# Experts of a small transformer stack: from every expert on every token to sorted pairs of token and chosen expert

## The reference

```python
comb = jnp.sum(jax.nn.one_hot(top_i, E) * top_w[..., None], axis=2)   # top 2 of E = 8, by a distance to 8 centroids
h = jax.nn.gelu(jnp.einsum('bnd,edf->bnef', x, W1) + b1)              # d = 128, f = 512
y = jnp.einsum('bnef,efd->bned', h, W2) + b2
out = jnp.einsum('bne,bned->bnd', comb, y)
```

## Time and profile before

| | |
|---|---|
| median of three runs | 763.6 us (761.05 to 763.6) |
| profiled execution | span 757.7 us; its own time is not given apart from the three runs |
| PE busy | 660.7 us, 87% of the span |
| DVE, ACT, POOL busy | 514.1, 342.2, 151.8 us |
| attention 0, experts with what is merged into them, attention 1 from its step 1 | 0 to 248.5, 248.5 to 506.7, 506.7 to about 700 us |

### The profile page before, as it was taken

One profiled execution on the slowest core, in us unless ns is written; L12 is line 12 of the kernel. 1 busy time (PEld: TensorE's weight loads), 2 busy tenths in 40 slices (PEclk: granted clock), 3 DMA queues, 4 the chain that ended last, 5 costly groups with the idle time before them and its releaser, 6 DMA issues.

```text
span 757.7 us, 13009 instructions
## 1 busy us (share of the span) xinstructions
PE 660.7 (87%) x5007; PEld 464.5 (61%) x5007; DVE 514.1 (68%) x1313; ACT 342.2 (45%) x472; POOL 151.8 (20%) x145
## 2 busy tenths in 40 slices
PE   1478889999989899999999998999989899998664
PEld 0333556565655699898998785775555655555443
DVE  6578776777743536658537467777786778666993
ACT  1110566656575444433444432335546455674221
POOL 5301010100011010010021301302203010345764
PEclk9995999999999999999999999999999999999985
DMA  5405876454320000000000200211211211000000
GB/s 152 126 22 147 173 218 132 85 141 75 66 55 14 1 1 1 1 1 1 1 1 1 63 1 12 75 23 28 83 42 27 65 45 35 25 12 1 14 15 28
DMA packets 29325, 38.07 MB, mean 50 GB/s; under 512 B 3719, under 2 KB 23185, under 8 KB 29265
## 3 DMA queue, kind: packets, MB, share of 16 engines
q1 hardware_dynamic: 29265, 37.25, 20.3%
HBM read 26.33 MB, written 10.88 MB: 49 GB/s over the span
## 4 chain that ended last, share of the span: by engine, by line
PE 64%; DVE 25%; issue 5%; ACT 3%; POOL 1%; DMA 0%; POOLq 0%; DVEq 0%; ACTq 0%
PE ps L989 14%; PE ps L486 9%; PE ps L444 7%; DVE mx L663 6%; PE ps L465 6%; PE ps L979 4%; PE ps L512 3%; PE ps L981 3%; PE ps L980 3%; DVE xn L926 3%; PE ps L447 2%; ACT pT L557 1%; PE ps L494 1%; PE ps L469 1%; DVE x L1063 1%
## 5 line engine op out<-in xcount | busy, mean ns | idle before, releaser
L663 DVE TENSOR_REDUCE mx<-ps 128x1 f32<-128x384 f32 (+3 forms) x352 | 215.5, 637 | 72.5 <-PE ps L447 70.4
L557 ACT ACTIVATE pT<-ps 128x1024 f32<-128x1024 f32 x160 | 162.1, 1023 | 86.9 <-PE ps L469 71.9
L1024 ACT ACTIVATE pT<-ps,b1c 128x512 f32<-128x512 f32 x128 | 87.8, 687 | 129.6 <-PE ps L981 128.7
L989 PEld LDWEIGHTS ps<-w_sb,pT 128*128 128x128 f32 x1024 | 132.2, 191 | 11.8 <-issue 1.3
L989 PE MATMUL ps<-w_sb,pT 128*128 128x128 f32 x1024 | 135.5, 275 | 0.0
L447 PE MATMUL ps<-mask_qk,identb 128*128 128x128 bf16 (+2 forms) x352 | 90.2, 256 | 0.0
L444 PE MATMUL ps<-stA 96*128 96x128 bf16 (+3 forms) x256 | 69.6, 332 | 19.2 <-DVE mx L663 14.3
L486 PE MATMUL ps<-pT,vA 128*32 128x512 f32 (+3 forms) x1024 | 77.9, 439 | 0.7 <-ACT pT L557 0.7
L1063 DVE SCALAR_TENSOR_TENSOR x<-ps,comb,x 128x128 f32<-128x128 f32 x128 | 36.0, 344 | 58.4 <-PE ps L989 58.3
L444 PE MATMUL ps<-kA,stA 96*128 96x128 bf16 (+3 forms) x256 | 63.7, 304 | 12.8 <-DVE mx L663 11.6
L979 PE MATMUL ps<-x_hi,w_hi 128*128 128x512 f32 x128 | 62.9, 491 | 1.2 <-DVE w_lo L1045 1.0
(11 more groups left out here) (232 smaller groups left out, 964.1 us busy)
## 6 DMA issues: line engine op xcount, KB each, us to landing
stA<-stack_scratch SPq DMA_DIRECT2D x48, 192.0 KB, 3.4
stB<-stack_scratch SPq DMA_DIRECT2D x48, 192.0 KB, 4.5
stack_scratch<-part SPq DMA_DIRECT2D x12, 384.0 KB, 3.2
w_sb<-in_L_ffn_W_dram SPq DMA_DIRECT2D x16, 256.0 KB, 5.6
stack_scratch<-part SPq DMA_DIRECT2D x12, 256.0 KB, 3.1
stack_scratch<-part SPq DMA_DIRECT2D x12, 128.0 KB, 3.1
x<-in_L_attn_z_dram SPq DMA_DIRECT2D x4, 256.0 KB, 4.4
out_dram<-x SPq DMA_DIRECT2D x4, 256.0 KB, 2.3
```

Source lines behind the costliest of these rows:

```text
L557: act.activation(dst_, src, ACT.Exp, scale=SCALE).then_inc(a["ex"], 1)
L663: nc.vector.tensor_reduce(mx[:, g % 2, qb, heads[0]:heads[0] + nh], ps[:, S_BANK[n % 2], 0:nh * w].rearrange("p (h k) -> p h k", h=nh), AX ...
L989: last = pe.matmul(ps[:, ST_BANK[1] + m % 2, f * P:(f + 1) * P], hT[:, (m % 2) * FC + c, f * P:(f + 1) * P], w2_sb[:, e, c, :], start=(c = ...
L1024: act.activation(hT[:, (m % 2) * FC + f, :], ps[:, ST_BANK[0] + n % 2, :], ACT.Gelu, bias=b1c[:, e * FC + f:e * FC + f + 1]).then_inc(M["g ...
```

## The change

The tokens are taken in two halves of 8 tiles (batches 0 and 1, then 2 and 3). Each half has 2,048 pairs of token and chosen expert. They get slots in an order sorted by expert, each expert's slots filled up to a multiple of 128; that is at most 16 + 7 = 23 tiles of 128 slots (`NTL`), and 23 are always run. The place of each pair is computed on DVE and PE ("CNT", "RANK", "POS"), POOL writes the normed tokens to their slots in DRAM by 16 indirect DMAs of 128 rows x 512 B a half ("SCAT"), SP loads the tiles one by one ("XG"), and POOL fetches each token's two results by 16 indirect DMAs a half ("GATH"); "COMB" on DVE adds them to x. A tile is turned ("XTT"), split on DVE, multiplied by W1 of its expert ("H", now with the tokens as the fixed side, and a fourth product for the bias), turned again ("HT") and multiplied by W2 ("Y", with a fifth product for the bias). The expert of a tile is known only on the chip, so PE loads 23 registers a half ("REG") and takes the weights at register addresses. W1 is split once, for all experts, in step 4 of attention 0, which needs W1 through a DRAM copy of 2 MB made at the start; the slots in DRAM are filled once beforehand (1.5 MB). Routing of batch 0 moves into step 3 of attention 0, of batch 1 into step 4, of batches 2 and 3 into the first 12 of the 49 rounds of experts; the weights of the last layer are quantized in rounds 12 to 24. The tail and step 0 of attention 1 stand alone.

```diff
+HALVES = 2
+TH = NT // HALVES
+NTL = 2 * TH + E - 1
+XG, YB = 4, 3
+def routing_order(b):
+    o = [(n, b, 0, 0) for names in ROUTING for n in names]
+    if b % 2:
+        o += [(n, b // 2, 0, 0) for n in ("CNT", "RANK", "POS", "SCAT")]
     return o
+def experts_order():
+    rounds = []
+    last = HALVES * NTL
+    for k in range(-2, last + 1):
+        o = []
+        for hf in range(HALVES):
+            if k + 2 == hf * NTL:
+                o += [("REG", hf, 0, 0)] + [("XG", hf * NTL + n, 0, 0) for n in range(XG)]
+        if k + 2 < last:
+            o.append(("XTT", k + 2, 0, 0))
+        if 0 <= k + 1 < last:
+            o.append(("H", k + 1, 0, 0))
+        if 0 <= k < last:
+            o.append(("HT", k, 0, 0))
+        if k >= 1:
+            o.append(("Y", k - 1, 0, 0))
...
+        for hf in range(HALVES):
+            if k - 1 == (hf + 1) * NTL - 1:
+                o.append(("GATH", hf, 0, 0))
...
+    o += merged(flat(rounds[:12]), of("M", routing_order(2) + routing_order(3)))
...
+    o += merged(flat(rounds[12:NTL + 2]), weights)
+    at = NTL + 2
+    o += flat(rounds[at:at + 4])
+    for t in range(TH):
+        o += rounds[at + 4 + t] + of("M", [("COMB", 0, t, 0)])
...
+    o += merged(flat(rounds[at:]), of("A1", first1[2:]))
+    start = steps1[0].index(("LN", 2, 0, 0))
+    o += of("A1", steps1[0][:start]) + of("M", [("COMB", 1, t, 0) for t in range(NB)]) + of("A1", steps1[0][start:])
...
+            elif name == "REG":
+                pe.wait_ge(M["pos"], b + 1)
+                for k in range(NTL):
+                    tiles[b * NTL + k] = pe.value_load(tid_i[0:1, b, k:k + 1], min_val=0, max_val=(E - 1) * F)
...
+                whi = w_hi[:].rearrange("p e f -> p (e f)")[:, bass.ds(tiles[n], F)]
+                wlo = w_lo[:].rearrange("p e f -> p (e f)")[:, bass.ds(tiles[n], F)]
+                pe.matmul(bank, x_hi[:, n % 2, :], whi, start=True, stop=False)
+                pe.matmul(bank, x_hi[:, n % 2, :], wlo, start=False, stop=False)
+                pe.matmul(bank, x_lo[:, n % 2, :], whi, start=False, stop=False)
+                pe.matmul(bank, hot[:, hf, k:k + 1].broadcast_to([P, P]), b1r[:], start=False, stop=True).then_inc(M["h"], 1)
...
+            elif name == "SCAT":
+                pool.wait_ge(M["pos"], b + 1)
+                pool.wait_ge(ld_fill, 32)
+                if b:
+
+                    pool.wait_ge(M["xtt"], b * NTL)
+                for t in range(TH):
+                    for k in range(2):
+                        g_.indirect_dma_start(xs_d, bass.IndirectOffsetOnAxis(ap=pos_i[:, b, k, t:t + 1], axis=0),
+                                              xe[:, t, :], None).then_inc(scat, 16)
```

More of the change, by code:

```diff
@@ L202, in network_order @@
     before, after = upto(of("A0", first0[2:]), ("A0", "LN", 1, 0, 0))
[L203 to L206, removed]
+    o += before + setup("ROWS", "COLS", "CENT", "CENTP", "CENTT", "CNORM") + after + setup("ONES", "LOAD")
+    o += of("A0", steps0[0]) + setup("BROWS") + merged(of("A0", steps0[1]), [("SETUP", "LOADE", e, 0, 0) for e in range(E)]) + of("A0", steps0[2])
@@ L208, in network_order @@
+    start = 3 * len(steps0[B - 1]) // 8
+    o += of("A0", steps0[B - 1][:start]) + merged(of("A0", steps0[B - 1][start:]), of("M", routing_order(0)))
     start = len(steps0[B]) // 8
[L209 to L214, removed]
@@ L215, in network_order @@
-    tail = of("A0", steps0[B + 1])
-    weights = [("SETUP", n, c, 0, 0) for c in range(3) for n in ("QW", "QV", "TW")]
-    o += of("M", [("WS", 0, 0, 0)]) + tail[:1] + merged(head, tail[1:]) + experts[0] + merged(experts[1], weights)
-    plain, beside = upto(experts[2], ("M", "H", 2, 6, 0))
-    plain, norm = upto(plain, ("M", "H", 2, 4, 0))
-    more, last = upto(experts[3], ("M", "H", 3, 3, 0))
-    o += plain + merged(norm, of("A1", first1[:2])) + merged(beside + more, of("A1", first1[2:]))
@@ L223, in network_order, with flat @@
-    o += merged(last, of("A1", steps1[0]))
+    weights = [("SETUP", "WS", e, 0, 0) for e in range(E)]
+    o += of("A0", steps0[B][:start]) + merged(of("A0", steps0[B][start:]), merged(of("M", routing_order(1)), weights))
+    o += of("A0", steps0[B + 1]) + setup("LOADF")
+    rounds = [of("M", r) for r in experts_order()]
+    def flat(lists):
+        return [step for r in lists for step in r]
+    o += merged(flat(rounds[:12]), of("M", routing_order(2) + routing_order(3)))
+    weights = [("SETUP", n, c, 0, 0) for c in range(3) for n in ("QW", "QV", "TW")]
@@ L378, in network, with loaded @@
         for layer in range(2):
-            a = {n: sem(f"{n}_{layer}") for n in both + rotary * layer}
-            for n in ("loadA", "loadB", "mload"):
-                a[n] = [sem(f"{n}{g}_{layer}") for g in range(G)]
-            A.append(a)
+            A.append({n: sem(f"{n}_{layer}") for n in both + rotary * layer})
+        loads = {n: [sem(f"{n}{g}") for g in range(G)] for n in ("loadA", "loadB", "mload")}
         STORES = (6, 3)
         NLA = (2, 1)
+        def loaded(layer, b):
+            return 16 * (NLA[0] * B * layer + NLA[layer] * (b + 1))
         def attention_sync(sp, layer, name, b, g, u):
@@ L451, in attention_tensor @@
                 if u == 0:
-                    pe.wait_ge(a["loadB"][g], 16 * NLA[layer] * (b + 1))
-                    pe.wait_ge(a["mload"][g], 16 * (b + 1))
-                    pe.wait_ge(ld_fill, 16)
+                    pe.wait_ge(loads["loadB"][g], loaded(layer, b))
+                    pe.wait_ge(loads["mload"][g], 16 * (B * layer + b + 1))
+                    pe.wait_ge(ld_fill, 32)
+                if n == 0 and layer:
+                    for read in ("ge", "hT", "yb", "xsplit"):
+                        pe.wait_ge(M[read], HALVES * NTL)
                 if n >= 2:
@@ L547, in attention_scalar @@
                     act.wait_ge(a["pv"], i - 1)
+                if n == 0 and layer:
+                    act.wait_ge(M["y"], HALVES * NTL)
+                    for r in range(YB):
+                        act.wait_ge(st_y[r], 16 * uses(HALVES - 1, r, YB))
                 act.wait_ge(a["st"], n + 1)
```

475 lines of the change are left out of this document (294 added, 181 removed).

## The result

The changed kernel took 804.6 us (median of 4 runs, 803.1 to 805.2). The kernel before took 762.3 beside it (760.8 to 763.6). The ratio is 1.056 (interval 1.053 to 1.060), so the change cost 42 us where 16 had been forecast; the forecast range went from 740 to 818. The profiled execution has a span of 802.4 us.

The account below looks back on a forecast made before the run. PE alone was taken to bound the experts stage. 90 us less PE work, paid back by scatters, lost cover, gathers and coupled waits, put the first "ST" at 523 against 506.7: span 774, forecast 780 us, range 740 to 818.

Parts of the forecast that it names:

- hidden behind the scatter: After the tail, PE's 23 register loads, 0.5 us each, end at 279, covered by the first scatter up to 0.76 each.
- the scatter can begin at 260: First scatter: routing of batch 0 ended at 246.8 before; with the placing of pairs and 13 us of lateness, start at 260.
- the bound of 10 us: Attention 0's step 3 with batch 0's routing: between 1.4 and 10 us longer by spare busy time; 7 taken.
- What follows is the same work: From attention 1's first "ST" (506.7 us before) to the end, the work is unchanged; only that event's time was forecast.
- The 79 us for tiles 0 to 22: First half's tiles: rounds 0 to 11 take 46 us, to 331; rounds 12 to 22 take 33 us, to 364.
- The 46: Rounds 0 to 11: chain of two routings at 21 us per batch, less the first norm, plus placing 6: 46 us.
- The price of an indirect DMA: In scatters and gathers, POOL needs 1.2 us for each, taken from its smallest fixed-cost operation; sixteen take 19.2 us.
- cheap DMAs: Rival: POOL needs only 0.74 us per indirect DMA, in three places of sixteen: 758, or 743 at 0.43; chance 0.25.
- one at a time: Rival: indirect DMAs don't overlap, 2.2 us or more each: 828 and up, 871 at 3.1; chance 0.06.
- products at register addresses and register work: Tiles were put at 2.5 us on PE; rival: register work and register-addressed products add 32 us, to 812; chance 0.12.
- The idle stretch of the second scatter: Between the halves, nothing covers PE while the second scatter runs and lands: 25 us, to 389.
- the wait of ACT for POOL's rotary sum: Attention 1's step 0: POOL's gathers delay its rotary sum to 23 where about 13 is asked: 10 us.

Follow-up runs that it names:

- e5: Changed kernel run again with no edit, in a session without held signals: 786.0 us, 1.034 of the kernel before.
- e9: Changed kernel run again with no edit, in a session with held signals: 805.2 us, 1.057 of the kernel before.
- e16: Changed kernel run once more with no edit, in another session with held signals: 804.5 us, 1.057 of the kernel before.
- e10: Changed kernel with the first half's 16 indirect gathers as plain loads by SP (rows in wrong order), with held signals: 789.6 us.
- e11: Changed kernel with the first half's 16 indirect gathers as plain loads issued by POOL (rows in wrong order), with held signals: 785.4 us.
- e13: Changed kernel with the first half's gathers issued one for each tile of the second half, with held signals: 790.3 us.
- e7: Changed kernel with the first batch's routing moved back from step 3 to step 4 of attention 0: 792.5 us, 1.042 of the kernel before.
- e18: As e17, with the routing's first block of small DVE operations cut into three pieces: 760.2 us, 1.000 of the kernel before.
- e6: Changed kernel with a scratch for each half and register loads of both halves two a tile: 763.9 us, 1.004 of the kernel before.
- e17: Changed kernel with own scratches, registers two a tile, spaced first-half gathers, last gathers in two groups, second scatter pausing for tiles: 758.2 us, 0.996 of kernel before.
- e12: Changed kernel with own scratches, spread registers, split last gathers, first-half gathers two a tile, part of attention 1's step 0 merged with tiles: 784.9 us, 1.033.

## Why the prediction was wrong

The direction was right, and so was the mechanism as far as it went. Stage by stage the forecast can be laid beside the four profiles of the changed kernel (us from the first event of each row to the next; the last row's forecast is the 251 us that followed 506.7 before):

| stage | forecast | e5, nothing held | first result | e9 | e16 |
|---|---|---|---|---|---|
| start to first scatter | 260 | 269.5 | 268.8 | 270.0 | 269.9 |
| to tile 0 turned | 25 | 23.3 | 31.6 | 29.3 | 29.6 |
| tiles 0 to 22 | 79 | 78.8 | 78.6 | 80.0 | 79.0 |
| second scatter, to tile 23 | 25 | 23.5 | 23.6 | 23.4 | 23.6 |
| its tiles, to the last product | 77 | 77.8 | 88.9 | 89.1 | 89.8 |
| to the first "ST" | 57 | 57.3 | 57.5 | 57.3 | 56.7 |
| rest | 251 | 254.8 | 253.4 | 253.9 | 254.1 |
| span | 774 | 785.0 | 802.4 | 803.0 | 802.7 |

**The step that failed** is one that the prediction did not have: that indirect DMAs in a row cost other engines something. It costed them by POOL's time and by their landing, and put what PE loses beside them at nothing. In the first profile they also held PE's signals: 8.3 us at the first scatter and 11.1 at the gathers, 19.4 of the 28.4 us by which the span was missed. e5 (the same program without the hold, 18.6 us less), e10 and e11 (without the indirect form) and e13 (without the row) show it. Beside the second scatter, where PE is idle, nothing was lost, and beside the last gathers nothing either in these four, since the stage waits for POOL's rotary sum. In a session without the hold the kernel was 25.5 us slower than the one before, for 16 forecast.

At the first scatter the hold undid a cover: "hidden behind the scatter" was said of the register loads. In the first profile PE came to them late, after the tail's ACT copy and the last addition had been held:

```profile
277.51 0.60 ACT L670 ACTIVATE oT<-ps 128x512 f32<-128x512 f32 x1 [5.97 <-remote]
...
291.76 0.69 DVE L766 TENSOR_TENSOR x<-ps,x 128x512 f32<-128x512 f32 x1 [11.86 <-remote]
```

PE's last "PV" had ended at 274.0. The loads then ran to 300.2 us. In e9 and e16 PE came to them at 278.0 and 277.9, 1.7 us later than in e5, and the loads themselves were slow (PE's sequencer: least, median and longest ns, first and last start; of the first profile, of e5 and of e9):

```profile
L1095 PEldq TENSOR_LOAD <-tid_i x23: 3/301/493, 283.3 to 299.6; - x23
```

```profile
L1095 PEldq TENSOR_LOAD <-tid_i x23: 295/304/494, 276.3 to 290.8; - x23
```

```profile
L1095 PEldq TENSOR_LOAD <-tid_i x23: 3/301/698, 278.0 to 298.5; - x23
L1095 PEldq SEQ_ASSERT  x23: 4/18/1395, 278.8 to 299.1; - x23
```

From one load to the next, with two register operations behind it, it is 14.5 / 22 = 0.66 us in e5, 16.3 / 22 = 0.74 in the first profile and 20.5 / 22 = 0.93 in e9; steps of 18 ns took up to 1.4 us there, in the last part of the scatter. So what was lost at the first scatter was PE's own time in its list, and not only signals to others. I had assumed 0.5, with cover up to 0.76. The Trainium skill ("DMA: Bandwidth & Descriptors", Latency and other measured facts) puts such a load at about 0.6 us at least; the trace has 0.66 from one to the next, and 0.30 for the load's own record.

**The second miss** is the start, 9 us, a term of the sum that was too small. "With CNT, RANK and POS behind it in the same order, and 13 us of lateness, the scatter can begin at 260" counted the placing of pairs as hidden work. It is hidden for PE, but the scatter waits for it:

```profile
262.62 0.21 DVE L1191 TENSOR_TENSOR counted<-chosen 128x64 bf16<-128x64 f32 x1
...
268.29 0.18 DVE L1238 TENSOR_SCALAR tid_i<-tid 128x23 int32<-128x23 f32 x1
```

These are 5.9 us, priced at zero on that path. The other 3 are the routing's own lateness, 15.3 us at its end in place of 13. Step 3 of attention 0 grew by 14.6 us, not 7: the bound of 10 us was made of busy times, and DVE's work indeed grew by about 7. But a block of small operations of the routing (216.1 to 219.4 us) stands ahead of the steps that split the group's maxima into parts (`mpart`), and PE waits for these and then runs its next products at the lower clock (the first two rows are DVE's, then PE's):

```profile
216.09 0.16 DVE L1263 TENSOR_SCALAR r<-r 128x4 f32<-128x4 f32 x1
...
219.47 0.17 DVE L746 TENSOR_SCALAR mpart<-mx 128x16 bf16<-128x16 f32 x1
...
220.33 0.48 PE L562 MATMUL ps<-identb,mpart 128*12 128x128 bf16 x3 [3.46 <-DVE mpart L749]
...
220.72 3.67 PE L554 MATMUL ps<-pT,vA 128*32 128x512 f32 x29
```

32 of these products take 2.36 us at the higher clock level (271.60 us; granted clock 1.00 there, 0.60 from 220.0 to 224.3). Of the 7.6 us above my figure only some 2 reached the scatter; what took up the rest in step 4 wasn't isolated. e7 and e18 show that moving the block wins back step 3, that cutting it wins back 2 us of it, and neither any of the time. "What follows is the same work" was true of the work and 2 to 4 us short on its time, in step 1 of attention 1; no run isolates that.

**What came out by luck.** The 79 us for tiles 0 to 22 are two errors that cancel: tiles 0 to 11 took 50.3 us in e5, to the turning of tile 12 at 343.1, for 46 forecast, and the others 28.5 for 33. The 46 don't follow from their terms either: 42 less a norm of 4.2 plus 6 are 43.8.

**What held.** The price of an indirect DMA, 1.2 us assumed, is 1.27:

```profile
270.33 0.97 POOL L1322 DMA_INDIRECT pairs_scratch<-vraw,pos_i  x1 [0.30 <-issue]
271.61 0.96 POOL L1322 DMA_INDIRECT pairs_scratch<-vraw,pos_i  x1 [0.31 <-issue]
```

The nearest row, POOL's smallest operation with a fixed cost, came close, and SP's issue of 0.74 did not; the rivals of cheap DMAs and of one at a time are out. The Trainium skill ("DMA: Bandwidth & Descriptors", Anatomy of one DMA) gives a cost by which sixteen in a row are an estimated 34 us if none overlaps; they take 20.2 here, so they overlap. A tile takes 2.46 us in place of the 2.5 assumed, so products at register addresses and register work add nothing that shows, and that rival is out too:

```profile
411.78 1.06 PE L1133 MATMUL ps<-w_sb,pT 128*128 x8
...
414.24 1.06 PE L1133 MATMUL ps<-w_sb,pT 128*128 x8
```

The idle stretch of the second scatter (22.0 us of PE) came as forecast, and e6 gives it back. So did the wait of ACT for POOL's rotary sum behind the last gathers: in e5 the sum starts 22.0 us after the last product, for 23 forecast.

## What to carry to other kernels

Price an indirect DMA twice: by POOL's 1.27 us for each, and by what stands beside it. Put sixteen in a row only where PE has nothing to do, as at the second scatter here, or leave a pause of a microsecond or two after each (e13), and write sorted halves to buffers of their own, so that the next scatter can start as soon as its addresses are known (e6). When work is moved under another engine's cover, look for a chain that runs through it: the places were cheap for every engine and still stood, link by link, on the path to the scatter. And run a kernel with indirect DMAs more than once, in separate sessions, before a difference of 2% is given a cause.

## What was not expected of the hardware

Beside rows of indirect DMAs on POOL (one each 1.27 us), what PE had finished reached ACT, DVE and, in e17, POOL late, with waits of about 1 to 12 us in the changed kernel and up to 15.8 in e12, from about 4 us after the first DMA until about 3 us after the last. PE's own register loads halted in the same way. It was so in the sessions of the first result, e9 to e12, e13 to e16 and e17 with e18, and in the two others never, with the same program (786.0 against 804.5 to 805.2 us). The kernel before, which has no indirect DMAs, did not change (760.2 to 762.3). Plain DMAs from POOL, 0.54 us apart and by the same queue, did not do it. What decides between the two sorts of session is open, and so is the mechanism.

The Trainium skill ("DMA: Bandwidth & Descriptors", SWDGE vs HWDGE vs iDMA) says that GpSimd writes the descriptors of its DMAs to rings in SBUF; no run here shows whether that has to do with it.
